# Moving two of the eight tiles of a normalisation from ScalarE to GpSimd in the first stage of a graph kernel

## The reference

```python
h = relu((x - mean(x)) / sqrt(var(x) + eps))
z = (h - mean(h)) / sqrt(var(h) + eps)      # goes to z_table in DRAM
```

## Time and profile before

| | |
|---|---|
| median of 3 runs | 3555.48 us |
| the profiled execution's own time | 3554.38 us |
| its span in the profile | 3552.5 us |
| first stage, to the first instruction of the second on GpSimd | 330.2 us |
| groups of nodes in the first stage | 49 |

### The profile page before, as it was taken

One profiled execution on the slowest core, in us unless ns is written; L12 is line 12 of the kernel. 1 busy time (PEld: TensorE's weight loads), 2 busy tenths in 40 slices (PEclk: granted clock), 3 DMA queues, 4 the chain that ended last, 5 costly groups with the idle time before them and its releaser, 6 DMA issues. The chain is left out here.

```text
span 3552.5 us, 56630 instructions
## 1 busy us (share of the span) xinstructions
PE 2248.5 (63%) x13730; PEld 1803.6 (51%) x13730; DVE 2280.3 (64%) x9173; ACT 1722.7 (48%) x4075; POOL 2301.1 (65%) x2429
## 2 busy tenths in 40 slices
PE   0002777777777773799999999997443442455554
PEld 0002667766667762566666666665333332444444
DVE  8886666666666664677877787775111111678778
ACT  8994333333333331678887888886111111344343
POOL 5554777777777771555555555551777775777776
PEclk9998999999999995899999999999555555555555
DMA  6553233333333332233333333341566664456676
GB/s 204 177 176 94 82 101 92 91 101 91 91 101 91 91 101 62 65 105 107 107 100 102 108 104 102 101 109 67 124 129 130 132 131 113 118 149 152 144 147 133
DMA packets 253888, 401.93 MB, mean 113 GB/s; under 512 B 56515, under 2 KB 165456, under 8 KB 253728
## 3 DMA queue, kind: packets, MB, share of 16 engines
q1 hardware_dynamic: 183670, 265.77, 25.2%
q0 software_dynamic: 63424, 133.57, 18.6%
q10 hardware_dynamic: 6682, 1.46, 0.2%
HBM read 241.74 MB, written 160.29 MB: 113 GB/s over the span
## 5 line engine op out<-in xcount | busy, mean ns | idle before, releaser
L1159 POOL DMA_INDIRECT agg<-rows,at_n x392 | 388.8, 992 | 144.4 <-issue 111.1
L1651 POOL DMA_INDIRECT aggc<-rows,at_nc x392 | 398.8, 1017 | 113.2 <-issue 104.8
L628 POOL DMA_INDIRECT zs<-z_table,at_s x392 | 381.0, 972 | 112.9 <-issue 104.7
L628 POOL DMA_INDIRECT zd<-z_table,at_d x392 | 375.0, 957 | 119.4 <-issue 105.7
L1476 POOL DMA_INDIRECT h2s<-h_table,at_s x392 | 372.8, 951 | 113.2 <-issue 90.9
L1224 PE MATMUL p_f<-z_t,w_t 128*128 128x512 f32 x784 | 377.4, 612 | 64.1 <-ACT act L1294 64.0
L1529 PE MATMUL p_sum<-h2s,same 128*128 128x129 f32 x784 | 208.1, 438 | 307.8 <-DMA h2s<-h_table,at_s 244.4
L1235 PE MATMUL p_f<-w_t,act 128*128 128x128 f32 x3136 | 383.8, 278 | 0.0
L1235 PEld LDWEIGHTS p_f<-w_t,act 128*128 128x128 f32 x3136 | 361.2, 192 | 22.2 <-issue 22.2
L1529 PEld LDWEIGHTS p_sum<-h2s,same 128*128 128x128 f32 x784 | 173.3, 318 | 342.5 <-issue 264.8
L1516 DVE TENSOR_SCALAR same<-dst_sb,dst_g 128x128 f32<-128x128 uint16 x392 | 84.0, 303 | 400.8 <-DMA dst_sb<-dst 392.5
(11 more groups left out here) (317 smaller groups left out, 6471.9 us busy)
## 6 DMA issues: line engine op xcount, KB each, us to landing
rows<-rows_sb SPq DMA_DIRECT2D x49, 576.0 KB
h_table<-h2b SPq DMA_DIRECT2D x49, 516.0 KB, 2.9
rows<-rows_sb SPq DMA_DIRECT2D x49, 516.0 KB
xa<-in_x_dram SPq DMA_DIRECT2D x49, 512.0 KB, 3.8
z_table<-za SPq DMA_DIRECT2D x49, 512.0 KB, 2.9
dst_sb<-dst SPq DMA_DIRECT2D x98, 256.0 KB
xb<-in_x_dram SPq DMA_DIRECT2D x49, 512.0 KB, 4.0
x_table<-x1b SPq DMA_DIRECT2D x49, 512.0 KB, 4.7
```

The costliest lines, as they stand in the source:

```text
L628: pool.indirect_dma_start(out=to[:, slot, k], out_offset=None, in_=z_table, in_offset=bass.IndirectOffsetOnAxis(ap=at[:, slot, k:k + 1], a ...
L1159: pool.indirect_dma_start(out=agg[:, ring, k], out_offset=None, in_=rows0, in_offset=bass.IndirectOffsetOnAxis(ap=at_n[:, ring, k:k + 1], ...
L1651: pool.indirect_dma_start(out=agg[:, slot, k], out_offset=None, in_=rows1, in_offset=bass.IndirectOffsetOnAxis(ap=at_n[:, slot, k:k + 1], ...
```

## The change

GpSimd gets a third part in each step, for group g-2: it waits for `norm_ready[1]` of that group and for the z buffer, and does tiles 5 and 6 of z, each with one `tensor_scalar`; the second raises the new semaphore `zp_ready`. This stands behind the two powers of the step. ScalarE does tiles 0 to 4, VectorE tile 7 as before. ScalarE's h of group g and SyncE's store of z wait for `zp_ready` too.

```diff
-            WAYS, ZA = 4, 7
+            WAYS, ZA, ZD = 4, 5, 7
 ...
+                        sp.wait_ge(zp_ready, g + 1)
+                        hold(sp, held)
 ...
-                        for k in range(ZA, G):
+                        for k in range(ZD, G):
 ...
+                def normed(g, slot, use):
+                    pool.wait_ge(norm_ready[1], g + 1)
+                    at_least(pool, z_out[slot % 2], 16 * (2 * use + slot // 2))
+                    hold(pool, held)
+                    for k in range(ZA, ZD):
+                        last = nc.gpsimd.tensor_scalar(z_sb[:, slot % 2, k], h_sb[:, slot % 2, k], norm[:, slot, 2, k:k + 1],
+                                                       norm[:, slot, 3, k:k + 1], ALU.mult, ALU.add)
+                    last.then_inc(zp_ready, 1)
+
-                def half(new, mid):
+                def half(new, mid, old):
 ...
                     if mid:
                         power(mid[0], mid[1], 1)
-                pipeline(pool, NGN, 2, half, WAYS)
+                    if old:
+                        normed(*old)
+                pipeline(pool, NGN, 3, half, WAYS)
 ...
                         at_least(act, za_ready, g - 1)
+                        at_least(act, zp_ready, g - 1)
```

More of the change, by code:

```diff
@@ L260, in build @@
                 [s(f"a_{name}{n}") for n in range(2)] for name in ("bn_done", "aggr_done", "var_ready", "rstd_ready", "norm_ready"))
-            h_ready, za_ready, zd_ready, stats_kept = s("a_h_ready"), s("a_za_ready"), s("a_zd_ready"), s("a_stats_kept")
+            h_ready, za_ready, zd_ready, zp_ready, stats_kept = s("a_h_ready"), s("a_za_ready"), s("a_zd_ready"), s("a_zp_ready"), s("a_stats_kept")
             def nodes_a_sync(sp):
```

## The result

The changed kernel takes 3658.78 us, the median of 4 runs (3640.09, 3641.51, 3676.04 and 3680.19), against 3555.39 us of 4 runs of the kernel before: a ratio of 1.0288, 95% interval 1.0241 to 1.0336. It is slower, by 3633 - 3555 = 78 us in the forecast and by 103 us in the median; the range of 3614 to 3685 us held it. The four runs lie in two pairs 37 us apart, 85 us and 123 us above the kernel before. The execution with the profile is one of the upper pair (3680.19 us, span 3678.3).

The account below looks back on a forecast made before the run. ScalarE was taken to set the first stage's pace; the change closes a 7.64 us loop: 47 x (7.64 - 5.995) + 0.6 = 78 us longer, so 3633 us, range 3614 to 3685 us.

Parts of the forecast that it names:

- The loop: First stage: h of g waits for GpSimd's z tiles queued behind the second norm's power; 7.64 us a round against 5.995.
- power 1.64: Loop term on GpSimd: the power of the second norm of group g-1, 1.64 us.
- two tiles 0.80: Loop term on GpSimd: the two z tiles of group g-2, 0.40 us each, 0.80 us for both.
- signal 0.04: Loop term: the signal to ScalarE after the z tiles, 0.04 us.
- h 3.18: Loop term on ScalarE: eight tiles of h of group g, 3.18 us.
- from h to the next power: Loop term: end of h to GpSimd's next power, with `bn_stats`, `bn_aggr`, eps and their signals, 1.98 us.
- The bound from the affine select: GpSimd's 128x128 affine select, 0.29 us, as guide from below; 0.1 us added for two scalars gives 0.40 us a tile.
- What lies beside the loop: First stage: ScalarE 5.17 us, VectorE 5.71, GpSimd 4.1, all under 7.64; SyncE's stores and the buffers priced at nothing.
- The edge loads' 0.6 us: GpSimd's edge-list loads in step 3 make the power of group 2 0.6 us late, once.
- The end of the stage: Behind the power of group 48 all goes as before, up to the second stage; priced at nothing.
- "Nothing of later stages changes.": Stages after the first: all keep their length, so they add nothing to the forecast.
- Rival A: First stage: tiles finish before h is due, VectorE bounds at 5.71 us a group; 13 us less, 3542 us; chance 0.05.

Follow-up runs that it names:

- second profile: The kernel before, run again unchanged on another chip: 4094.2 us in one run, against a median of 4111.9 us there.
- the last trial: The kernel before with one VectorE wait added between `mixed` and `basec` in the last stage: 3548.37 us against 3559.44, ratio 0.9971.

## Why the prediction was right

*The loop.* Right in its parts and in its order, term by term (prediction, then measured): power 1.64, 1.64; two tiles 0.80, 0.88 (203.17 to 204.05); signal 0.04, 0.12; h 3.18, 3.18; from h to the next power 1.98, 1.98 (207.35 to 209.33). Sum 7.64 and 7.79, and 7.82 over the 47 rounds of the power (21.43 to 388.97 us), with the turns of the loop. The bound from the affine select for a tile on GpSimd was a good guide: 0.43 to 0.45 us against 0.29, so some 0.15 us a tile, not 0.1, stand for the two scalars and whatever else differs between the two instructions. The signal I had taken from VectorE to ScalarE; from GpSimd to ScalarE it is three times as long. Tiles and signal together are 0.16 us a round, 7.5 of the 8 us between 78 and 86.

*What lies beside the loop.* Right: ScalarE and VectorE at 65 and 71 in 100, as 5.17 / 7.8 and a VectorE that waits for h would have it; nothing on SyncE or in the buffers bound a round. The edge loads' 0.6 us are there too, as 0.5: the power of group 2 starts at 29.72 us, where 21.43 + 7.79 would be 29.22.

*The end of the stage.* Priced at nothing, and it cost 0.9 us (from the power of group 48 to the second stage it is 27.7 us, 26.8 before). The last four tiles, of groups 47 and 48, came beside VectorE's fill and took 5.76 us, but the preparation covered most.

*"Nothing of later stages changes."* This step failed in the profiled run and, by its time, in one more of the four. The last stage took 39.9 us more in the profiled one, by the gathers that VectorE's instructions hold: `mixed` follows the copies without a wait in 19 of its 49 rounds, against 4 of 49 in the kernel before. The kernel before can have as many (31 in its second profile), but by their times it had not in its 4 runs beside the changed one nor in its 11 beside the last trial, on chips of the same speed. Whether the changed kernel has them more often, by another phase at the stage's start or by chance, is open: on the other three chips every profile had them, of the kernel before and its variants as of the changed one.

*The number.* The first stage alone makes it 3555.4 + 86.5 = 3642 us, and the lower pair of runs lies at 3641. That the median of 3659 us, with half of the last stage's surplus in it, and even the run of 3680 us are inside the range is luck: the range was opened upwards for dearer tiles, which the tiles were not.

*Rival A* was sized wrongly. The relief, once it reaches the pace, is worth 4 us in the rounds and not 13, because VectorE's round is 5.905 us with its turn. The sum didn't rest on it.

## What to carry to other kernels

Before work is handed to an engine that is idle half of the time, follow its instruction stream: what stands ahead of the new work, and what that waits for. Ready work behind an instruction that needs the newest result of the pipeline closes a loop through every wait on it; here the place cost 0.96 us a round and the work itself 0.43 us a tile, and putting the work one place further ahead took all of it back. A period read from one round of an unrolled loop leaves out the turn: take it over a whole turn at least.

## What the runs showed of the hardware

- A gather that GpSimd issues beside a VectorE instruction that reads two tiles of SBUF is held, and ends 0.8 us behind it. Where VectorE had waited directly before the first of two such instructions, it was held for that one only (132 of 132, records of up to 2.0 us; 0.95 to 1.19 us where the instruction was cut into pieces of 0.36 us). Where it had not, the gather was held through the second as well (273 of 279): 0.94 us became 2.88 us beside two of 1.21 us and up to 3.58 us beside eight of 0.36 us, but 1.97 us where a wait of VectorE's stood between the two.
- The Trainium skill (SBUF — State Buffer, section on who interferes with whom) has a VectorE instruction with two inputs in SBUF contend with a GpSimd instruction that reads SBUF; the gathers held here agree with that. The same section reports that `tensor_tensor` was not seen to stall the DMAs that GpSimd issues, and speaks of a hold for the whole of one instruction; here `tensor_tensor` did hold them (2.88 us for 0.94), and over two instructions in a row.
- The two engines slow each other on other instructions too: VectorE's eps of 0.17 us took 0.31 beside GpSimd's third tile, and GpSimd's three tiles took 5.93 us beside a fill of 2.02 us and the casts and other instructions behind it, 1.30 us within the loop. Beside `bn_stats` and `bn_aggr`, which read one tile, GpSimd's tiles kept their 0.44 us.
- A signal from GpSimd to ScalarE took 0.11 to 0.12 us from the end of the record to the start of the next, from VectorE to ScalarE 0.04 us.
